# A three-layer graph attention network and a tensor-product convolution on one core: order of VectorE's per-step work, the linear logit part as a 33rd column, counters held per loop body

## The reference

```
xl = x @ Wl + bl;  xr = x @ Wr + br                 # (n, 8, 32)
e = leaky_relu(xl[src] + xr[dst], 0.2)
logits = einsum('ehc,hc->eh', e, att)
p = exp(logits - segment_max(logits, dst)[dst])
alpha = p / (segment_sum(p, dst)[dst] + 1e-16)
out = segment_sum(xl[src] * alpha, dst).mean(heads) + bias
x = batchnorm(leaky_relu(out, 0.01) + x)            # last layer: out + x
```

## Time and profile before

| what | value |
|---|---|
| runs (3) | median 7016.35 us, 7012.04 to 7020.23 |
| profiled execution | span 7015.3 us, 173867 instructions |
| PE busy | 5813.7 us (83%) |
| DVE busy | 5946.5 us (85%) |
| ACT busy | 3310.9 us (47%) |
| POOL busy | 4860.6 us (69%) |
| chain that ended last | PE 43%, issue 17%, DVE 16%, DVEq 9%, POOL 9%, DMA 3% |
| DVE: L1198 `u`, L1206 `lr`, L1225 `px`, L1239 `acc` | 1012.3, 1012.3, 991.0, 606.2 us |
| POOL: L503 gathers | 2808 of 1028 ns on average, 2885.2 us |
| granted clock of TensorE, mean | 0.922 of 2.4 GHz |

### The profile page before, as it was taken

How to read it: one execution, slowest core, us unless ns; L and a number is a source line. 1 busy time by engine, 2 the same in 40 slices (tenths; PEclk the granted TensorE clock), 3 DMA queues, 4 the chain that set the end, 5 groups by cost and what they waited for, 6 DMA issues and landing times.

```text
span 7015.3 us, 173867 instructions
## 1 busy us (share of the span) xinstructions
PE 5813.7 (83%) x27916; PEld 4277.5 (61%) x27917; DVE 5946.5 (85%) x12084; ACT 3310.9 (47%) x10977; POOL 4860.6 (69%) x7291
## 2 busy tenths in 40 slices
PE   0589898888579898898757898998864999999998
PEld 0366666665546666666445666666644777777776
DVE  7689999998669999899767999999977888888888
ACT  0155555556125555555513555555541444444444
POOL 1788888783288888788048887888603777777775
PEclk8789999999689999999959999999985999999999
DMA  2211111111011111111001111111201111111111
GB/s 84 64 34 37 36 36 39 34 36 16 6 39 36 36 36 39 34 36 36 7 16 38 36 39 33 37 36 36 34 0 32 34 34 35 34 34 33 34 35 29
DMA packets 214546, 237.88 MB, mean 34 GB/s; under 512 B 72925, under 2 KB 195902, under 8 KB 213950
## 3 DMA queue, kind: packets, MB, share of 16 engines
q1 hardware_dynamic: 93630, 163.53, 7.7%
q0 software_dynamic: 120704, 72.40, 6.7%
HBM read 222.44 MB, written 13.20 MB: 34 GB/s over the span
## 4 chain that ended last, share of the span: by engine, by line
PE 43%; issue 17%; DVE 16%; DVEq 9%; POOL 9%; DMA 3%; POOLq 1%; ACT 1%; ACTq 0%; SPq 0%
PE psum L673 16%; PE psum L658 12%; PE psum L804 3%; PE psum L660 3%; POOL xg L558 3%; DVEq L1232 3%; PE psum L646 2%; POOL xg L503 2%; PE psum L818 2%; DMA xg<-table,idx 2%; DVE u L1198 2%; DVE acc L1239 2%; DVEq L1028 1%; DVE xs L1573 1%; PE psum L649 1%
## 5 line engine op out<-in xcount | busy, mean ns | idle before, releaser
L503 POOL DMA_INDIRECT xg<-table,idx x2808 | 2885.2, 1028 | 712.3 <-PE psum L649 250.7
L658 PE MATMUL psum<-wz,xt 128*128 x5928 | 1823.3, 401 | 49.8 <-ACT xt L929 49.7
L673 PE MATMUL psum<-px,oh 128*128 128x272 f32 x5616 | 1643.6, 417 | 255.9 <-DVE acc L1239 240.7
L673 PEld LDWEIGHTS psum<-px,oh 128*128 128x128 f32 x5616 | 961.0, 191 | 650.0 <-DVE acc L1239 433.8
L658 PEld LDWEIGHTS psum<-wz,xt 128*128 128x128 f32 x5928 | 1001.5, 197 | 406.9 <-issue 65.4
L1198 DVE SCALAR_TENSOR_TENSOR u<-psum,atts 128x512 f32<-128x512 f32 x1482 | 1012.3, 683 | 220.1 <-PE psum L660 219.4
L558 POOL DMA_INDIRECT xg<-table,idx x936 | 902.2, 964 | 394.0 <-issue 219.6
L1206 DVE TENSOR_REDUCE lr<-u 128x16 f32<-128x512 f32 x1482 | 1012.3, 685 | 107.7 <-DVE u L1198 58.9
L1225 DVE TENSOR_TENSOR px<-xs,pg 128x528 f32 (+1 forms) x1404 | 991.0, 706 | 80.1 <-PE psum L673 40.2
L858 ACT ACTIVATE dist<-iota_f,ndloc 128x128 f32<-128x128 f32 x2808 | 974.3, 394 | 95.0 <-PE psum L673 72.1
L876 ACT COPY lin<-psum 128x16 f32<-128x16 f32 x1482 | 254.7, 172 | 1284.2 <-DVE u L1198 1283.4
(11 more groups left out here) (273 smaller groups left out, 7330.2 us busy)
## 6 DMA issues: line engine op xcount, KB each, us to landing
dr<-dlocs SPq DMA_DIRECT2D x468, 192.0 KB
xg<-table,idx POOLq DMA_INDIRECT x3744, 2.4
at<-w_rows SPq DMA_DIRECT2D x156, 192.0 KB, 3.1
fl<-flags SPq DMA_DIRECT2D x30, 576.2 KB
flags<-fl SPq DMA_DIRECT2D x10, 576.2 KB, 3.2
table<-xn SPq DMA_DIRECT2D x3, 784.0 KB, 3.8
xp<-keys SPq DMA_DIRECT2D x5, 385.0 KB, 4.4
u<-keys SPq DMA_DIRECT2D x5, 385.0 KB, 4.4
```

What stands on the lines that cost most here:

```text
L503: nc.gpsimd.indirect_dma_start(out=xg[:, s % S6, t, 96:128], out_offset=None, in_=table, in_offset=bass.IndirectOffsetOnAxis(ap=idx[:, s, ...
L658: pe.matmul(out_z, xt[:, r, e * P:(e + 1) * P], wz[:, bass.ds(l, 1), :].rearrange("p o z -> p (o z)"), start=True, stop=False)
L673: last = pe.matmul(agg_ps(r), oh[:, s % 3, e, :], px[:, s % 3, e, :], start=(e == 0), stop=(e == 1))
```

## The change

- DVE's order in a step becomes `u`, `px`, `lr`, `acc`, `oht`; the block numbers of the body are loaded behind its first `px`.
- `u` gets a 33rd column per head: ACT copies the 8 linear columns there (still L876's copy), and the reduction runs over 33 elements and writes `lg` (or `self_l`) itself. `lr`, `lin`, the additions and the semaphore `l_done` are gone; `lr`'s reduction waits for both `u` and ACT's copy.
- ACT does `linear` first in a step, before the one-hots.
- `brow` is laid out by body, eight numbers each. `blocks_from` loads the six numbers of a body with one load on PE and on DVE; the counts of each body are computed once (`pin`), and each wait adds a constant.
- The second network and the ends of groups still load single numbers, from the new layout.

```diff
+def pin(engine, count):
+    return count if isinstance(count, int) else engine.snap(count)
...
-        brow = sb("brow", [1, NSP], I32)
+        brow = sb("brow", [1, (NBODIES + 2) * 8], I32)
...
-        u = sb("u", [P, 2, 2, HC])
-        lr = sb("lr", [P, 2, J, 2, H])
-        lin = sb("lin", [P, 2, J, 2, H])
+        u = sb("u", [P, 2, 2, H, C1])
...
+        def blocks_from(engine, t, j, n):
+
+            regs = [engine.alloc_register(f"block{next(names)}") for _ in range(n)]
+            engine.load(regs, brow[0:1, t * 8 + j:t * 8 + j + n] if isinstance(t, int) else brow[0:1, bass.ds(t * 8 + j, n)])
+            return [engine.snap(r, donate=True, min_val=0, max_val=BLOCKS - 1) for r in regs]
...
             def pe_body(l, g, i, a, b, ends_group):
                 k0 = (g * BODIES + i) * S6
-                t = l * NBODIES + g * BODIES + i
+                gathered = pin(pe, (l * NBODIES + g * BODIES + i) * 32)
+                z0 = pin(pe, l * ZS + k0)
+                m0 = pin(pe, l * NS + k0)
+                added = pin(pe, l * AGGS + g - 1 + k0 - GS)
+                fronts = min(S6, S6 - 4 if ends_group else S6) if a else 0
+                at_blocks = blocks_from(pe, g * BODIES + i + 1, 0, fronts) if fronts else None
                 for s in range(S6):
...
+            def linear(zn, r):
+
+                act.wait_ge(u_done, AHEAD + zn + 1)
+                op.copy(u[:, r, :, :, C], z_ps(r, HC, ZW)).then_inc(lin_done, 1)
...
                 for s in range(S6):
+                    if a:
+                        linear(z0 + s, s % 2)
                     if b and (s + 1 < S6 or not (ends_group if ends_b is None else ends_b)):
-                        weights_of(l, g - 1, i, s + 1)
-                    if a:
-                        linear(l, k0 + s, s % 2, (g * BODIES + i) * 2 + s // J, s // J, s % J)
+                        weights_of(m0 + (s + 1), k0 + (s + 1 - GS), i, s + 1)
                     if a and (s + 3 < S6 or not ends_group):
-                        keep(l, g, i, k0 + s + 3, s + 3)
+                        keep(z0 + (s + 3), s + 3)
...
+            def over_channels(zn, r, to):
+
+                v.wait_ge(u_done, AHEAD + zn + 1)
+                v.wait_ge(lin_done, AHEAD + zn + 1)
+                op.tensor_reduce(to, u[:, r], AX.X, ALU.add).then_inc(r_done, 1)
...
                 for s in range(S6):
+                    if a:
+                        weighted(l, z0 + s, s % 2)
                     if b:
+                        weigh_rows(m0 + s, ring, i, s)
+                    if b and s == 0:
+                        at_blocks = blocks_from(v, (g - 1) * BODIES + i, 0, S6)
                     if a:
+                        over_channels(z0 + s, s % 2, logits_at(i * 2 + s // J, s % J))
+                    if b and (s > 1 or not starts_group):
+                        add_sums(m0 + (s - 2), added + (s - 2), s % 2, at_blocks[s])
+                    if a and (s + 5 < S6 or not ends_group):
+                        one_hot_t(loaded, z0 + (s + 5), s + 5)
```

More of the change, by code:

```diff
@@ L25 @@
+import itertools
 from contextlib import ExitStack
@@ L1034, in _ @@
             op.memset(zero1[:], -2.0)
+            op.memset(brow[:], 0)
             op.memset(cnt, 0.0)
@@ L1181, in _ @@
             op.tensor_scalar(real[:, BLOCKS - 1:BLOCKS], iota_p[:], float(N - (BLOCKS - 1) * P), None, ALU.is_lt)
-            for counter in (u_done, r_done, l_done, oht_done, px_done, acc_done, gb_done, h_done):
+            for counter in (u_done, r_done, oht_done, px_done, acc_done, gb_done, h_done):
                 v.sem_inc(counter, AHEAD)
@@ L1208, in logits @@
-            def logits(l, n, c, steps, to):
-                v.wait_ge(r_done, AHEAD + l * ZS + n + 1)
-                v.wait_ge(lin_done, AHEAD + l * ZS + n + 1)
-                op.tensor_tensor(to, lr[:, c, 0:steps].rearrange("p j e h -> p (j e) h"),
-                                 lin[:, c, 0:steps].rearrange("p j e h -> p (j e) h"), ALU.add).then_inc(l_done, 1)
-            def chunk_logits(l, g, i, half):
-                n = ((g * BODIES + i) * 2 + half) * J + J - 1
-                logits(l, n, half, J, lg[:, :, bass.ds(i * 2 + half, 1), :].rearrange("p k o h -> p (k o) h"))
@@ L1220, in weigh_rows, with logits_at @@
+            def logits_at(c, j):
+                return lg[:, 2 * j:2 * j + 2, bass.ds(c, 1) if not isinstance(c, int) else slice(c, c + 1), :].rearrange("p e o h -> p e (o h)")
+            def weigh_rows(m, ring, i, s):
                 r, c, j = s % 3, i * 2 + s // J, s % J
-                m = l * NS + k
                 v.wait_ge(xs_done, AHEAD + m + 1)
                 v.wait_ge(agg_done, AHEAD + m - 2)
-                rows = xs[:, bass.ds((l * GROUPS + g) % 2, 1), bass.ds(i * S6 + s, 1), :, :].rearrange("p o q e c -> p (o q e) c")
+                rows = xs[:].rearrange("p g s q c -> p (g s) q c")[:, bass.ds(ring + s, 1), :, :].rearrange("p o e c -> p (o e) c")
@@ L1242, in dve_body @@
                 k0 = (g * BODIES + i) * S6
-                ahead = None
+                z0 = pin(v, l * ZS + k0) if a else None
+                loaded = pin(v, (l * NBODIES + g * BODIES + i) * 16) if a else None
+                if b:
+                    m0 = pin(v, l * NS + k0 - GS)
+                    added = pin(v, l * AGGS + g - 1 + k0 - GS)
+                    ring = pin(v, (l * GROUPS + g - 1) % 2 * GS + i * S6)
                 for s in range(S6):
-                    r = s % 2
-                    adds = b and (s > 1 or not starts_group)
+                    if a:
+                        weighted(l, z0 + s, s % 2)
@@ L1276, in dve_group @@
                     dve_body(l, g, i, a, b, False, False)
-                ahead = dve_body(l, g, n - 1, a, b, False, True)
-                whole = a and b and n == BODIES
-                if whole:
-                    last = block_at(g * GS - 1)
-                if a:
-                    chunk_logits(l, g, n - 1, 1)
+                dve_body(l, g, n - 1, a, b, False, True)
                 if a and b:
@@ L1286, in dve_group @@
                 if b:
-                    k = min(g * GS, NS) if isinstance(g, int) else g * GS
-                    add_sums(l, g - 1, k - 2, 0, ahead if whole else block_at(k - 2))
-                    add_sums(l, g - 1, k - 1, 1, last if whole else block_at(k - 1))
+                    t = min(g * BODIES, NBODIES) if isinstance(g, int) else g * BODIES
+                    last = blocks_from(v, t, 0, 2)
+                    for s in range(2):
+                        add_sums(l * NS + t * S6 - 2 + s, l * AGGS + g - 1 + t * S6 - 2 + s, s, last[s])
             def early_places(l, g, steps):
                 for s in steps:
-                    one_hot_t(l, g, 0, g * GS + s, s)
+                    one_hot_t((l * NBODIES + g * BODIES) * 16, l * ZS + g * GS + s, s)
             open_f, open_b = fl[:, CW + 1:2 * CW + 1], fl[:, 2 * CW + 1:3 * CW + 1]
```

184 lines of the change are left out of this document (76 added, 108 removed).

## The result

The changed kernel takes 6886.35 us (median of 4 runs, 6882.44 to 6888.89) against 7016.19 us of the kernel before (4 runs, 7012.04 to 7020.23): the ratio is 0.9815, with a 95% interval of 0.9801 to 0.9829. It is faster, by 130 us where 246 were forecast: 6770 us was said, in a range of 6650 to 6940. The measured time lies above the 6840 us at which the prediction let its own mechanism end, in the part of the range that was there for rival A. The profiled executions span 6882.2 and 7015.3 us, the granted clock is 0.922 in both.

What follows compares the result with a forecast made beforehand. The PE and DVE chain was taken to bound paired groups (148.3 us), POOL next at 139.5. Gains of 65 + 8 + 7 + 2 = 82 us a layer, times three 246: 7015.3 - 246 + 1.1 = 6770 us, range 6650 to 6940.

Steps and rivals of the forecast that it cites:

- rival A: POOL's gathers collide more with `px`: POOL needs 145 us per group, gain 34 us a layer, 6914 us; chance 0.17.
- DVE's step: DVE's step inside a body of six steps falls from 2.48 us to 2.38 to 2.39 by the new order.
- Rival C: DVE's new order gains nothing, or the strided write costs its gain: step stays 2.5 us, 6806 us; chance 0.06.
- rival D: DVE's channel sum `lr` waits for ScalarE's `lin` copy: at 0.5 us per step, 7286 us; chance 0.05.
- The boundary of a body: Between six-step bodies: DVE hole 0.5 us, PE hole 0.9, the larger counts; body 15.2 us (14.3 to 16.1), 16.9 before.
- PE's hole of 0.9 us: Branch, counts and load before PE's first transposes of a body, 2.0 us, 1.1 covered: 0.9 left, bounds 0 and 1.8.
- What is late next: Paired groups: PE and DVE path falls to 135 us, so POOL binds at 139.5 per group, needing no stop during the maxima.
- 1.4 for `px` coming more often: Added to POOL's own 138.1 us per group for more frequent `px` and imperfect meeting, giving 139.5.
- the forecast's own band: Floors of 137 to 142.5 us per paired group, giving 6710 to 6840 us; the forecast itself had chance 0.56.
- Group 9: Last front to last front, 113.6 us before: POOL's 36 steps at 2.9 us need 105, gain 8 us a layer.
- The last 36 steps: Last aggregation steps of a layer: from 1.57 us to 1.3 each, ScalarE late next, gain 7 us a layer.
- The second network: Same number of block loads and same order; with the setup's memset and copy counted 0, bounds -10 and +10 us.

Runs made afterwards that it cites:

- the run with half of the product: Changed kernel with DVE's rows' product `px` made for only four of eight heads, a probe that leaves out work: 6727.52 us, ratio 0.9588 to the kernel before.

## Why the prediction was right or wrong

- **DVE's step**: right. 2.37 us for 2.38 to 2.39 said, `px` 0.60 behind `u`, the sum 0.61 behind `px`. Rival C did not hold. The rule of the Trainium skill that the prediction quotes for it (VectorE: DVE Perf Modes, The DRAIN you can't avoid) is only half of what the section says: it adds that a next op that is not held starts earlier. With that addition it does not say that the edit gains nothing. The trace agrees with the addition, `px` starting 0.60 us behind the start of a `u` of 0.68 us; what makes an instruction held no run here tests. The old order shows what the order is worth beside the column: with the old one the step of the changed kernel is 0.42 us longer. The prediction had this as rival D, but priced the order at 0.12 us per step; it is what makes the column possible.
- **The boundary of a body**: 15.2 us said, 14.72 measured, inside 14.3 to 16.1. DVE's load of six took 0.81 us for the 0.8 chosen, and left 0.33 to 0.39 us of hole for 0.5 said. PE's hole of 0.9 us was not there, its lower bound was the truth. Its load of six takes 0.82 us, and at the end of an unheld body the transposes follow without idle time; only L685 waits, 0.23 us for `acc`:

```profile
L373 PEldq TENSOR_LOAD <-brow x354: 297/816/845, 223.4 to 4939.9; - x177
```

```profile
2491.44 0.38 PE L658 MATMUL psum<-ident,xg 128*128 128x128 f32 x2
2491.66 0.27 PE L662 MATMUL psum<-oht,x 128*96 128x256 bf16 x1
2492.16 1.19 PE L685 MATMUL psum<-px,oh 128*128 128x272 f32 x4 [0.23 <-DVE acc L1247]
```

- **What is late next**: right in the engine, wrong in the size, and here lies the miss. The step that failed is "it need not stop there. So POOL is late next: 139.5 us per group". Measured are 143.6: POOL's own part is 140.7 (1.2 more), and it does still stop, 2.9 us per group, at the start of a group, where PE is in the maxima and frees no gather buffer until 6.3 us behind the scan. 8 x (143.6 - 139.5) = 33 us per layer, the gain over the eight groups being 32 where 65 were said. The 2.9 us were the same in the run with half of the product, so a better body does not remove them. For POOL's own part the term "1.4 for `px` coming more often" should have been 2.0 over the 138.7 of eight groups, or 2.8 over the 138.1 of groups 2 to 8; it is the copies that meet `px`: index copies 209 to 259 ns, row copies 265 to 282, gathers unchanged at 1.03 us. Rival A looked for it in the gathers and at 145 us. That the time lies in the range is in part luck: the period of 143.6 us is outside the 137 to 142.5 of the forecast's own band, and the range took it in for the sake of rival A, whose mechanism is not what happened.
- **Group 9**: last front to last front 110.5 us (3168.5 to 3279.0), a gain of 3.1 where 8 were said. POOL waits 2.66 us for PE at its start here too; that this and its pace are all of the loss was not shown.
- **The last 36 steps**: 45.9 us instead of 54.1, a gain of 8.2 for 7; ACT is late next with steps of 1.34 us (1.3 said):

```profile
3330.29 0.69 ACT L875 ACTIVATE dist<-iota_f,ndloc 128x128 f32<-128x128 f32 x2
...
3331.63 0.69 ACT L875 ACTIVATE dist<-iota_f,ndloc 128x128 f32<-128x128 f32 x2
```

- **The sum**: in layer 1 the terms are 32 + 3 + 8 + about 3 for the rest, 47 us from its first front to that of layer 2, for 82 said. In layers 0 and 2 the eight groups gave 29 us each, so that the layers together gave about 130 us for 246. The second network, from its first product to the end, takes 1626.7 us for 1628.2, inside its bounds.
- **What each part brought**: the order alone 0.6% in the kernel before, but 5% in the changed kernel (1.0332 to 0.9815), so the parts can't be added; the column and the kept counts, on top of the order, the rest of 1.9%; the load once per body nothing. Whether the kept counts alone bring something was not tried. By the working the parts were credited as order 0.12 us a step, column 0.2 and the end, boundary the rest; the boundary's gain can't have come from the loads, since single ones per step gave 14.38 us a body.

## What to carry to other kernels

When an engine that runs ahead (here POOL, with its gathers) waits for the bound engine, divide its time without those waits by the units of work: this is the next floor, and the gain of any edit on the bound engine ends there. Take from its waits only those that will go: a wait that ends at a fixed place of the group, where the buffers are full and the consumer does something else, gets shorter only by the time that the engine comes later to it. Before an operand is split between two engines, put an independent instruction between the writer and the reader: the same kernel with the column was 1.9% faster than before with one and 3.3% slower without.

## What the runs showed of the hardware

- A DVE instruction (`px`, both inputs in SBUF) lengthens POOL's instructions that start while it runs. In the changed kernel such a gather takes 1.30 us on average (331 of 3744), another 0.98, and such an index copy of 128x2 elements 0.39, one that `px` does not meet 0.20. With `px` 0.44 instead of 0.70 us the mean of all index copies in the eight groups fell from 259 to 198 ns, that of the gathers from 1028 to 1003.
- One load of six block numbers takes 0.81 us on DVE and 0.82 on PE, single loads 0.30; spread over the steps the single ones show nowhere on DVE.
- The same kernel took 7014 to 7017 us in three sessions and 7763 to 7782 in three others, with nearly equal durations of its instructions and a mean granted clock of TensorE of 0.92 and of 0.88 to 0.90, and the change turned from 1.9% faster to 0.8% slower. A part of the difference, 950 us in the changed kernel, lies between the end of a TensorE product and the start of the VectorE instruction that waits for it; its cause is open.
- A hand-over from VectorE to ScalarE and back, with a ScalarE copy of 0.19 us, took 1.01 us from start to start of the VectorE instructions; an independent instruction started 0.60 us behind.
